# Row spectra kept on chip, and column transforms as 64-row tiles of TensorE, in a Fourier layer on one Trainium2 core

## The reference

```python
xn = _layernorm(x, norm1_w, norm1_b)
xf = jnp.fft.rfft2(xn.astype(jnp.float32), axes=(1, 2), norm='ortho')
xf = xf.reshape(B, h, w // 2 + 1, NB, BS)
w1c = jax.lax.complex(w1[..., 0], w1[..., 1])
b1c = jax.lax.complex(b1[..., 0], b1[..., 1])
o1 = jnp.einsum('bhwni,hwnio->bhwno', xf, w1c) + b1c
o1 = jax.lax.complex(jax.nn.relu(o1.real), jax.nn.relu(o1.imag))
xs = jnp.fft.irfft2(o1, s=(h, w), axes=(1, 2), norm='ortho')
xm = _layernorm(xs, norm2_w, norm2_b)
hdn = jax.nn.gelu(xm @ mlp_w1 + mlp_b1, approximate=False)
mlp_out = hdn @ mlp_w2 + mlp_b2
return xs + residual + mlp_out
```

## Time and profile before

| | us |
|---|---|
| median of 3 runs | 1189.72 (1187.06 to 1192.08) |
| the profiled execution, its own time | 1187.93 |
| its span | 1186.1 |
| PE busy in the span | 1068.2 (90%) |
| DVE, ACT, POOL busy | 804.3, 725.0, 352.8 |

### The profile page before, as it was taken

How to read it: one execution, slowest core, us unless ns; L and a number is a source line. 1 busy time by engine, 2 the same in 40 slices (tenths; PEclk the granted TensorE clock), 3 DMA queues, 4 the chain that set the end, 5 groups by cost and what they waited for, 6 DMA issues and landing times. The chain is left out here.

```text
span 1186.1 us, 25550 instructions
## 1 busy us (share of the span) xinstructions
PE 1068.2 (90%) x9064; PEld 816.2 (69%) x9064; DVE 804.3 (68%) x2102; ACT 725.0 (61%) x1325; POOL 352.8 (30%) x386
## 2 busy tenths in 40 slices
PE   2559999994799999999799999999999599999998
PEld 1249888882487888888555554654654388888887
DVE  4736555641768886776768689699698567666665
ACT  2646565651766667666677576567535266766665
POOL 1260021111322222221238437348157211111110
PEclk9869899996899999999899999999999699999999
DMA  6978699995300000000100000000000000000001
GB/s 138 284 184 159 147 186 182 169 196 155 93 6 0 0 0 0 0 0 0 47 1 1 1 1 1 1 1 1 1 1 0 1 14 27 27 27 27 27 27 40
DMA packets 140280, 64.26 MB, mean 54 GB/s; under 512 B 115856, under 2 KB 134960, under 8 KB 140192
## 3 DMA queue, kind: packets, MB, share of 16 engines
q1 hardware_dynamic: 132888, 37.42, 15.5%
q0 software_dynamic: 5664, 18.83, 6.1%
q10 hardware_dynamic: 1648, 6.91, 1.8%
HBM read 44.27 MB, written 12.58 MB: 48 GB/s over the span
## 5 line engine op out<-in xcount | busy, mean ns | idle before, releaser
L1093 PE MATMUL L_conv_ps<-w2hl,L_conv_hhi 128*128 128x384 f32 x768 | 228.0, 365 | 8.1 <-DVE X L993 7.5
L909 ACT ACTIVATE L_conv_hf<-L_conv_ps,L_conv_b 128x512 f32<-128x512 f32 x192 | 132.1, 688 | 150.9 <-PE L_conv_ps L1074 142.2
L983 DVE TENSOR_TENSOR L_conv_hlo<-L_conv_hf,L_conv_hhi 128x512 fp32r<-128x512 f32 x192 | 140.0, 744 | 103.4 <-ACT L_conv_hhi L918 101.1
L1093 PE MATMUL L_conv_ps<-w2hl,L_conv_hlo 128*128 128x192 f32 x768 | 188.3, 252 | 0.0
L862 POOL TENSOR_TENSOR X<-X,L_conv_b 128x192 f32 x128 | 72.4, 598 | 358.8 <-DVE L_conv_xn L968 358.8
L1208 POOL TENSOR_TENSOR sc_lo<-XS,sc_hi 128x512 fp32r<-128x512 f32 x96 | 141.6, 1490 | 115.6 <-ACT sc_hi L1284 115.6
L1093 PEld LDWEIGHTS L_conv_ps<-w2hl,L_conv_hhi 128*128 128x128 f32 x768 | 144.2, 188 | 14.7 <-DVE L_conv_hlo L983 7.2
L1093 PEld LDWEIGHTS L_conv_ps<-w2hl,L_conv_hlo 128*128 128x128 f32 x768 | 146.1, 191 | 0.0
L639 PE MATMUL psF<-spectrum,X 100*24 100x64 f32 x4352 | 128.4, 290 | 12.3 <-issue 9.0
L1284 ACT ACTIVATE sc_hi<-XS 128x512 fp32r<-128x512 f32 x144 | 87.2, 629 | 82.6 <-DVE XS L1341 29.3
L639 PEld LDWEIGHTS psF<-spectrum,X 100*24 100x24 f32 x4352 | 121.4, 121 | 21.8 <-issue 21.3
(11 more groups left out here) (146 smaller groups left out, 2147.9 us busy)
## 6 DMA issues: line engine op xcount, KB each, us to landing
X<-in_L_conv_w SPq DMA_DIRECT2D x136, 144.0 KB
XS<-in_x POOLq DMA_DIRECT2D x8, 768.0 KB, 7.0
rows_spectrum<-XS POOLq DMA_DIRECT2D x8, 768.0 KB, 4.3
d<-rows_spectrum ACTq DMA_DIRECT2D x8, 768.0 KB, 5.1
X<-in_x SPq DMA_DIRECT2D x8, 768.0 KB, 7.7
out<-X SPq DMA_DIRECT2D x15, 384.0 KB, 2.6
XS<-d POOLq DMA_DIRECT2D x59, 96.0 KB, 4.9
spectrum<-in_L_conv_mlp_w SPq DMA_DIRECT2D x2, 576.0 KB, 9.7
```

What stands on the lines that cost most here:

```text
L909: nc.scalar.activation(hf[:, m % 3, :], ps[:, RB + m % 2, :], gelu, bias=b1[:, m:m + 1]).then_inc(act1, 1)
L983: nc.vector.tensor_tensor(hlo[:, m, :], hf[:, m % 3, :], hhi[:, m, :].bitcast(F32), ALU.subtract).then_inc(h_lo, 1)
L1093: mm = pe.matmul(o, x, w, start=(m == 0 and n == 0), stop=(m == MT - 1 and n == 1), skip_group_check=True)
```

## The change

1. **The row spectra stay on chip.** X holds all 8 groups (d2 is a view of X). After each slab's copies SP issues 8 transfers of 16 rows x 6 KB, one for each group, from d1 into X, and before those of slab k it waits until all of slab k - 1 have landed (`arrived`). The write to HBM and the 8 reads are gone. The tables are reordered so that 16 adjacent partitions of d1 are one group, and each bin of a group takes 64 partitions of its own.
2. **The results go where the spectra were** (d3 is a view of d2): no buffer has to come free.
3. **The weight ring moves to XS**, shifted by one place. SP loads unit 0's pieces behind the transfers of slabs 5, 6 and 7.
4. **The scatters come at the end**, since XS holds the ring: SP issues 60 after the last weights, ACT 4, POOL none; the MLP's weights come behind them. X is reloaded whole, 8 x 768 KB, in the next block.
5. **Column transforms by single bins**: `columns` is 16 matmuls with a contraction over 64 partitions and 64 columns, taking lower and upper partitions in turn, each into its own bank; `inverse` is 4 matmuls of 64 x 64 by 384 for groups 1 to 7, one for each quarter of the array, so that ACT and DVE each do two copies of 64 partitions for one of 128. The weights' products, unit order and prefetch stay.

```diff
+    fwd_h = np.concatenate([fc[spread], fc[spread]])
...
+    ib = ic[halves][:, spread]
...
+    first = np.block([[real, z], [z, ib]])
+    inv_h = np.concatenate([np.concatenate([ib, ib]), first, np.block([[last, z], [z, z]]), np.block([[z, z], [last, z]])], 1)
...
-        F1 = nc.dram_tensor("rows_spectrum", [P, TPB, B * C], F32, kind="Internal").ap()
...
+        d2 = [X[:, B * g:B * (g + 1), :] for g in range(NG)]
+        d3 = [d2[g].rearrange("p b c -> p (b c)") for g in range(NG)]
+        def place(u):
+            return (u + RING - 1) % RING
+        Wt = [XS[0:HALF + NH, NT // RING * r:NT // RING * (r + 1), :].rearrange("p a c -> p (a c)").rearrange(
+            "p (k h o r) -> p k h o r", k=2, h=H, o=BS) for r in range(RING)]
         XT = 3
-        slab = [XS[:, B * k:B * (k + 1), :] for k in range(XT + 4)]
-        xt, xn, d1 = slab[0:XT], slab[XT:XT + 2], slab[XT + 2:XT + 4]
-        Wt = [X[0:HALF + NH, NT // RING * r:NT // RING * (r + 1), :].rearrange("p a c -> p (a c)").rearrange(
-            "p (k h o r) -> p k h o r", k=2, h=H, o=BS) for r in range(RING)]
+        slab = [XS[:, B * k:B * (k + 1), :] for k in range(XT + 3)]
+        xt, xn, d1 = slab[0:XT], slab[XT:XT + 2], [slab[XT + 2], sb("d1", [P, B, C])]
...
-        d2 = [sb(f"d2{k}", [P, B, C]) for k in range(2)]
...
+        def copies(g, half):
+            n = 2 * g + half + 1
+            return n if g == 0 else 2 * n - 2
...
+        def arrival(g):
+            return min(g, 2)
+        def arrived(eng, n, steps):
+            passed(eng, d2_in[n], 16 * steps * (1 if n < 2 else NG - 2))
         def scatter(eng, g, k):
             eng.dma_start(XS[g:P:NG, B * k:B * (k + 1), :].rearrange("p b c -> p (b c)"),
-                          d3[g % 2][k:P:TPB, :]).then_inc(sh.last_in[k] if g == NG - 1 else sh.rows_in[g % 2], 16)
+                          d3[g][k:P:TPB, :]).then_inc(sh.rows_in[k], 16)
...
-            for i in range(STEP):
-                sp.wait_ge(d1_done, 2 * TPB + 2 * i)
-                load_piece(0, i)
-            sp.wait_ge(d2_in[1], 16)
+            for k in range(TPB):
+                sp.wait_ge(d1_done, 4 * (k + 1))
+                for n in range(3):
+                    arrived(sp, n, k)
+                for g in range(NG):
+                    sp.dma_start(d2[g][k:P:TPB].rearrange("p b c -> p (b c)"),
+                                 d1[k % 2][P // NG * g:P // NG * (g + 1)].rearrange("p b c -> p (b c)")
+                                 ).then_inc(d2_in[arrival(g)], 16)
+                for i in {5: (0, 1), 6: (2, 3, 4), 7: (5, 6, 7)}.get(k, ()):
+                    load_piece(0, i)
...
-            def again(u, half):
-                r = u % RING
-                sp.dma_start(X[:, B * (2 * r + half):B * (2 * r + half + 1), :], x_v[2 * r + half]).then_inc(sh.x_back[r], 16)
-            for n, (u, half) in enumerate(itertools.product((UNITS - 4, UNITS - 3), range(2))):
-                sp.wait_ge(mixed, STEP * (UNITS - 2) + 2 * n + 1)
-                again(u, half)
-            for n, (dst, src) in enumerate(sh.mlp_loads("L0_conv_")):
-                sp.wait_ge(mixed, STEP * (UNITS - 1) + n + 1)
+            def ready(g):
+                sp.wait_ge(d3_v, copies(g, 1))
+                sp.wait_ge(d3_a, copies(g, 1))
+            ready(NG - 4)
+            for n, groups in enumerate((NG - 3, NG - 3, NG - 2, NG - 2)):
+                if n > 0:
+                    sp.wait_ge(mixed, STEP * (UNITS - 3 + n))
+                if n == 2:
+                    ready(NG - 3)
+                    for k in range(4):
+                        scatter(sp, NG - 3, k)
+                for g, k in itertools.product(range(groups), (2 * n, 2 * n + 1)):
+                    scatter(sp, g, k)
+            for g, slabs in ((NG - 2, range(TPB)), (NG - 1, range(0, TPB, 2))):
+                ready(g)
+                for k in slabs:
+                    scatter(sp, g, k)
+            for dst, src in sh.mlp_loads("L0_conv_"):
                 sp.dma_start(dst, src).then_inc(sh.raw_in, 16)
-            sp.wait_ge(d3_v, 2 * NG)
-            sp.wait_ge(d3_a, 2 * NG)
-            for k in (0, 3, 6):
-                scatter(sp, NG - 1, k)
...
-            for k in range(TPB):
-                if k + XT < TPB:
-                    load(k + XT)
-                pool.wait_ge(d1_done, 4 * (k + 1))
-                pool.dma_start(F1[:, k, :], d1[k % 2].rearrange("p b c -> p (b c)")).then_inc(f1_out[k % 2], 16)
+            for k in range(XT, TPB):
+                load(k)
             n_vectors = sh.load_vectors(pool)
-            for g in range(NG):
-                pool.wait_ge(d3_v, 2 * (g + 1))
-                pool.wait_ge(d3_a, 2 * (g + 1))
-                for k in range(TPB) if g < NG - 1 else (1, 4, 7):
-                    scatter(pool, g, k)
...
-                        passed(act, f1_out[s], 16 * (k // 2))
+                        for n in range(3):
+                            arrived(act, n, k - 1)
...
-            def spectrum_rows(g):
-                act.dma_start(d2[g % 2][:, :, :].rearrange("p b c -> p (b c)"), f1_r[g]).then_inc(d2_in[g % 2], 16)
-            for s in range(2):
-                act.wait_ge(f1_out[s], 16 * TPB // 2)
-            for g in range(2):
-                spectrum_rows(g)
...
-                act.wait_ge(hdft, u + 1)
+                act.wait_ge(hdft, 2 * (u + 1))
                 if u >= 2:
                     act.wait_ge(mixed, STEP * (u - 1))
-                v = ps[0:HALF, col_bank(u) + 1, :].rearrange("p (b r f) -> p r b f", b=B // 2, r=2)
-                for cut, of in slots(u):
-                    for part, n in itertools.product(range(3), range(NH)):
-                        scale = (ngm if part == 0 else gm)[:, of, n:n + 1]
-                        nc.scalar.activation(S[u % 2][0:HALF, part, n, B // 2:, cut], v[:, int(part != 1), :, cut], ACT.Copy,
-                                             scale=scale).then_inc(spread_a, 1)
+                v = ps[0:HALF, col_bank(u) + 1, :].rearrange("p (b r h) -> p r b h", b=B, r=2)
+                for part, n in itertools.product(range(3), range(NH)):
+                    scale = (ngm if part == 0 else gm)[:, half_of(u, 1), n:n + 1]
+                    nc.scalar.activation(S[u % 2][0:HALF, part, n, :, H:], v[:, int(part != 1)], ACT.Copy,
+                                         scale=scale).then_inc(spread_a, 1)
...
-                j = 2 * half + 1
-                act.wait_ge(inv_done, 4 * g + j + 1)
-                if g >= 2 and half == 0:
-                    act.wait_ge(sh.rows_in[g % 2], 16 * TPB * (g // 2))
-                nc.scalar.activation(d3[g % 2][:, 384 * j:384 * j + 384], ps[:, 7, 0:384], ACT.Copy).then_inc(d3_a, 1)
+                act.wait_ge(inv_done, 8 * g + 4 * (half + 1))
+                for to, fr, j in [(slice(0, P), slice(0, P), 1)] if g == 0 else [(upper, lower, 0), (upper, upper, 1)]:
+                    at = NH * HALF * (2 * half + j)
+                    nc.scalar.activation(d3[g][to, at:at + NH * HALF], ps[fr, 7, 0:NH * HALF],
+                                         ACT.Copy).then_inc(d3_a, 1)
...
-            for k in (2, 5):
+            act.wait_ge(d3_v, copies(NG - 1, 1))
+            act.wait_ge(d3_a, copies(NG - 1, 1))
+            for k in range(1, TPB, 2):
                 scatter(act, NG - 1, k)
...
-                pe.wait_ge(d2_in[g % 2], 16 * (g // 2 + 1))
+                arrived(pe, arrival(g), TPB)
                 if u >= 2:
                     spread_done(0 if u == 2 else u - 1)
-                at = col_bank(u)
-                for b in range(B):
-                    bank, col = at + b // 4, P * (b % 4)
+                for b, k in itertools.product(range(B), range(2)):
+                    out = ps[0:HALF, col_bank(u) + k, 2 * H * b:2 * H * (b + 1)]
                     if units[u] is None:
-                        for s in range(2):
-                            out = ps[0:HALF, bank, col:col + P].rearrange("p (r f) -> p r f", r=2)[:, :, H * s:H * (s + 1)]
-                            mm = pe.matmul(out, d2[0][:, b, HALF * s:HALF * (s + 1)], fwd_h0[:, P:], start=True, stop=True)
+                        mm = pe.matmul(out, d2[0][:, b, HALF * k:HALF * (k + 1)], fwd_h0[:, 2 * H:], start=True, stop=True)
                     else:
-                        s = units[u][1]
-                        mm = pe.matmul(ps[0:HALF, bank, col:col + P], d2[g % 2][:, b, HALF * s:HALF * (s + 1)],
-                                       fwd_h0[:, 0:P] if g == 0 else fwd_h[:, :], start=True, stop=True)
-                mm.then_inc(hdft, 1)
+                        table, s, rows = fwd_h0 if g == 0 else fwd_h, units[u][1], (lower, upper)[k]
+                        mm = pe.matmul(out, d2[g][rows, b, HALF * s:HALF * (s + 1)], table[rows, 0:2 * H],
+                                       start=True, stop=True)
+                    if b == B - 1:
+                        mm.then_inc(hdft, 1)
...
```

(74 more changed lines are left out.)

80 lines of the change are left out of this document (26 added, 54 removed).

## The result

The change makes the kernel **slower by 0.7%**: 1197.07 us in the median of 15 runs (1187.16 to 1200.51), against 1188.86 for the kernel before in 15 runs beside it (1184.16 to 1194.05); ratio 1.0068, 95% interval 1.0051 to 1.0085. The forecast was 1179.0, faster, with a range of 1163 to 1197; the time lies 0.07 us above the range's end. The profiled execution took 1196.19 us, its span 1194.4, against 1186.1 before: 8.3 more.

The account below looks back on a forecast made before the run. Bounds: the slabs' trip through HBM at the start, PE in the units, a PE stall under full DMA and POOL's drain at the end. +7.6 - 14.4 - 3.1 + 1 = -8.9, from 1187.9 to 1179.0 us, range 1163 to 1197.

Parts of the forecast that it names:

- Start: Row stage up to first products: SP's chain of slab transfers sets the pace, 7.6 us a slab; +7.6 us (+0.3 to +22.9).
- the term for the landing: Within a slab's 7.6 us at the start: 2.9 us for transfers to land, added to 4.7 of issuing.
- the skill's port rule: Slab transfers: 16 adjacent rows reach four ports, so 8 transfers take 7.2 us, not 4.7; some 17 us more over seven slabs.
- The transfers of slabs land late: Rival at the start, chance 0.22: landing 4.8 us in place of 2.9, columns start at 100, 15.3 us more, 1194 us.
- "near 85" and "95 or later": Signs in the profile: PE's first columns near 85 us would show the forecast right, at 95 or later wrong.
- Units: First products to the fifteenth unit's end: shorter columns and inverse give 9.9 us, fewer stalls 4.5; -14.4 us, a unit 9.6.
- the stalls: Of 9 us of stalls and slow clock in the units, half, 4.5 us, goes as DMA share falls to 0.8 (bounds 0 and 9).
- PE's waits for scaled copies: Sign of a wrong forecast in the units: if ACT's or DVE's slack went, the columns would be late next.
- End: Fifteenth unit to first row matmul: POOL's 9.37 us drain goes, SP's list eats most; 40.5 against 43.6, -3.1 us (-6 to +3.5).
- 60 scatters x 0.59 = 35.4: SP's list at the block's end: 60 scatters at 0.59 us an issue take 35.4 us of the 40.5.
- Next block: After the end: reloading 6.3 MB is covered; code fetched beside full DMA costs +1 us (0 to 6).
- The stall of the earlier trace: PE's 5.96 us stall at the end under full DMA; rival that it returns behind the reload, chance 0.10: 6 more, 1185.

Follow-up runs that it names:

- run 7: Changed kernel with the slab's transfers reading every eighth row in place of 16 neighbours, spectrum order wrong, for time alone: 1192.47 us, ratio 1.0046 to the kernel before.
- Run 1: Changed kernel without SP's wait for a slab's landing: semaphores split by slab parity, only ACT waits; 1185.72 us, ratio 0.9989 to the kernel before.
- run 6: Changed kernel with the columns' two loops exchanged, eight matmuls on the lower 64 rows, then eight on the upper: 1205.95 us, ratio 1.0155 to the kernel before.
- runs 3 and 4: 3: changed kernel with POOL issuing 24 of SP's 60 scatters early, 1187.68 us; 4: the same, POOL also issuing SP's four of the last group, 1192.14 us.
- run 2: Changed kernel with ACT also issuing the 8 scatters of the last group but one, SP 52 in place of 60: 1195.38 us, ratio 1.0059 to the kernel before.

## Why the prediction was wrong

**Start: wrong, and the largest miss** (+16.4, forecast +7.6). The mechanism was named: SP must wait for a slab's landing before it issues the next. The step that failed is the term for the landing: it was taken from the median, "2.9 in the median with quiet queues". But a wait for eight transfers is ended by the one that lands last. It was the eighth in every slab, issued 4.4 us after the first, and its landing took 6.9, 4.9, 5.7, 3.0, 3.9, 3.0 and 2.9 us in the first seven slabs, 4.3 in the mean. With 0.1 until SP issues again that is 4.4 + 4.3 + 0.1 = 8.8 a slab, the measured pace, where the forecast had 4.7 + 2.9 (it counted the last issue twice, since landing is counted from an issue's start). Seven times 1.2 make 8.4 of the 8.8 us missed. PE began 2.91 us behind the start of group 0's transfer of the last slab, where the forecast had 0.59 + 2.9. The 17 us more that the forecast set against this step from the skill's port rule rest on a misreading (run 7).

Run 1 shows that the wait is the cause. What makes the early slabs late can be read from the trace. POOL's queue issues loads of x, 768 KB each, in between:

```profile
31.11 0.88 POOL L404 DMA_DIRECT2D XS<-in_x  x1 [6.65 <-ACT XS L428]
...
44.25 0.88 POOL L404 DMA_DIRECT2D XS<-in_x  x1 [7.83 <-ACT XS L428]
53.53 0.88 POOL L404 DMA_DIRECT2D XS<-in_x  x1 [8.40 <-ACT XS L428]
```

The transfers issued just behind them are the late ones: the last four of slab 0, from 31.4 us on (6.2 to 6.9), the last of slab 1, at 44.6 (4.9), and the last of slab 2, at 53.9 (5.7). The other 18 of these slabs took 2.6 to 2.8, and from slab 3 on, with no load of x left, none took over 4.0. So x's loads are the likely cause; no run moved them. The direction of the source rows is a small part (run 7).

The rival "The transfers of slabs land late" named this, with the 4.8 of the earlier trace rows, which is the weights' traffic. Its 1194 us came nearest to 1197.07, in part by luck: it had the start at +22.9 (measured +16.4) and kept the end at -3.1 (measured +3.2), and these two misses cancel. Of the signs set down, first columns at 93.30 lie between "near 85" and "95 or later".

**Units: the steady unit right, the stalls not.** Columns were forecast at 1.4 and took 1.51, the inverse at 0.9 and took 0.80: two small misses that cancel, so that a unit took the forecast 9.6. Tiles overlap because neighbours stand on different halves (run 6). For the stalls, take the prediction's own subtraction: PE alone now needs 109.5 + 2.9 + 13 x 1.51 + 2 x 2.79 + 9 x 0.80 = 144.8 us, which leaves 5.4 of 150.2, against 9.0 before: 3.6 less, forecast 4.5. With 1.4 for the columns, 0.9 the other way for the inverse and 0.2 for group 0's that is the 1.6 us of difference. But 150.2 is the shortest of the eight profiles. By their mean, 153.7, the stretch gave 9.3 us, which the columns (4.0) and the inverse (5.3) account for, and 8.9 us of stalls are left where there were 9.0; PE's idle time that the profiles show is about 3 us before and in that mean. So the 4.5 us taken off for stalls are not borne out, though the DMA share fell as forecast. The kernel before has a single profile, so this stays likely and not shown. PE's waits for scaled copies, named as what might come next, did not come inside the steady units.

**End: the sign was wrong** (+3.2, forecast -3.1, bounds -6 to +3.5). The mechanism held: SP's list is the bound, POOL's drain is gone, PE's last units have cover (runs 3 and 4). The term "60 scatters x 0.59 = 35.4" was mis-sized: they took 42.35, 0.71 each. Starts are 0.63 apart even where nothing is long ((291.5 - 289.0) / 4 in the second row below), which makes some 2.5 us more in 60. And six issues take longer than 0.8 us, 4.5 more in all: five of 1.1 to 1.7 before 281 us, with other transfers in flight, and one of 0.88 at 284:

```profile
L335 SPq DMA_DIRECT2D XS<-X x5: 589/590/1733, 265.0 to 267.6; - x5
...
L335 SPq DMA_DIRECT2D XS<-X x5: 588/589/590, 289.0 to 291.5; - x5
```

The earlier trace rows came from three issues, too few to show either; the earlier trace rows with its 1208 ns maximum was the row that warned. Why a single issue takes 1.7 us was not tried. "MLP's weights 4 x 0.65" and the wait behind them held (2.41).

**Next block: the number right, the reason not** (+0.8, forecast +1 for code fetched beside full DMA). The stall of the earlier trace rows did not return, and the 0.8 us stand in the row stage's 64 matmuls:

```profile
298.82 23.75 PE L729 MATMUL psI<-XS,inv_w 128*128 128x384 f32 x64 [19.56 <-PEq L246]
...
292.03 22.95 PE L722 MATMUL psI<-XS,inv_w 128*128 128x384 f32 x64 [11.89 <-PEq L248]
```

(after, then before). Behind PE's wait of 19.6 us the granted clock was 0.50 in their first 5 us, the lower of its two levels (1.2 GHz), and 0.92 in the next 5; behind the 11.9 us before it was 0.58 and 1.00. 5 x (0.08 + 0.08) = 0.8 us: the time is the clock's, and the forecast's 1 us was luck.

In sum 8.8 + 1.6 + 6.3 - 0.2 = 16.5 us of miss in the stretches; the profiled execution of the changed kernel lies 1196.19 - 1179.0 = 17.2 over the forecast, and the other 0.7 are spread over the rest of the span. Two accidents of this one profile partly offset each other in it: its units are the shortest of eight, and its first slab, at 28.83, is the latest of all profiles (25.2 to 28.5 in the runs).

## What to carry to other kernels

Price a wait on a set of transfers by the latest of them under the traffic of its own moment, never by the median of quiet ones; if the wait only guards a buffer, split its semaphore by buffer and let the buffer's writer wait. A list of transfers on one queue costs its issues one after the other: once that list is the last thing in a block, share it among the queues that are idle, with POOL's share early, since its drain follows. When a change removes the bound (here POOL's drain), write down the next one's end time with its worst row, not its median. And do not credit fewer stalls from one profile before and one after: here eight profiles of the same units lay 7 us apart.

## What the runs showed of the hardware

- POOL's drain at a block's end took 7.1 to 9.4 us where it had issued transfers shortly before, and 3.4 where it had waited for its last to land before (75.9 us in the changed kernel); SP's took 0.1 to 0.4 and ACT's 0.4 in the rows shown, ACT's behind fresh transfers (0.65 behind 12 of them in run 2).
- The same 16-row transfer of 96 KB landed in 2.6 us at least from neighbouring rows, in 2.1 from every eighth row.
- With the next slab's transfers issued before a slab had landed, landing rose: the second slab's 8 took 6.5 to 8.8 us in run 1, 2.6 to 4.9 in the changed kernel.
- Issuing was 0.59 us as a rule, and up to 1.73 us for single ones; with POOL issuing at the same time SP's mean was 33.10 / 36 = 0.92 us, waits for readiness included.
- Two matmuls on 64 rows in alternating halves ran at 94 ns each, in the same half at 161 ns (1.51 and 2.57 us for 16). On all 128 rows 16 such matmuls took 2.86 us with the banks in turn and 2.87 without.
- After 19.6 us without matmuls PE's granted clock was 0.50 for the next 5 us and 0.92 in the 5 behind; after 11.9 us it was 0.58 and 1.00.
